# Two weighted rows of a token added on GpSimd instead of in TensorE's transposes, and another order at the end of an attention and expert kernel

## The reference

```python
x = x + xattn(layernorm(x), ctx)        # softmax(q k^T / 8) v, then Wproj and a bias
h = layernorm(x)                        # the second half, per token
probs = softmax(h @ gate_w.T); w2, i2 = top_k(probs, 2)
y = silu(h @ expert_w.T + expert_b)     # of experts i2 alone
x = x + (sum over the two of w2 * y[i2]) @ combine_w.T
```

## Time and profile before

| | |
|---|---|
| time, median of 3 | 1557.53 us (1556.89 to 1558.26) |
| the profiled execution | 1557.89 us, its span 1555.8 us |
| busy | PE 96%, DVE 83%, ACT 68%, POOL 60% |
| chain that ended last | PE 74%, DVE 14%, issue 5% |
| mean granted TensorE clock | 0.995 of full |

### The profile page before, as it was taken

The page is one execution under the profiler, slowest core; times in us unless marked ns, Lnnn a source line. Parts: engine busy times, 40 slices in busy tenths (PEclk is TensorE's granted clock), DMA queues, the critical chain, the costliest instruction groups (busy, mean ns, idle before and its releaser), DMA issues.

```text
span 1555.8 us, 38495 instructions
## 1 busy us (share of the span) xinstructions
PE 1492.6 (96%) x11680; PEld 1436.3 (92%) x11680; DVE 1289.1 (83%) x3129; ACT 1060.4 (68%) x2929; POOL 939.2 (60%) x1237
## 2 busy tenths in 40 slices
PE   6989999999999999999999999999999999999778
PEld 6889999999899999999899999989999999999767
DVE  7898888888888888888988888888888888877556
ACT  5766777777667766677667677667776766767545
POOL 4666666666555655687766555576676556655524
PEclk9999999999999999999999999999999999999989
DMA  6643433333577777445687777657888877877813
GB/s 194 194 149 96 120 96 96 96 96 101 165 227 232 215 222 219 120 127 145 189 246 237 207 221 226 177 159 227 246 243 242 243 215 238 267 224 226 292 58 109
DMA packets 181595, 287.78 MB, mean 185 GB/s; under 512 B 23696, under 2 KB 116880, under 8 KB 181136
## 3 DMA queue, kind: packets, MB, share of 16 engines
q1 hardware_dynamic: 170640, 255.94, 56.4%
q0 software_dynamic: 10752, 29.37, 6.0%
HBM read 156.51 MB, written 61.60 MB: 140 GB/s over the span
## 4 chain that ended last, share of the span: by engine, by line
PE 74%; DVE 14%; issue 5%; ACT 2%; POOL 2%; DMA 2%; SPq 0%; DVEq 0%; ACTq 0%; POOLq 0%
PE gen_ps L592 19%; PE qk_ps L592 17%; PE o_ps L592 10%; PE s_ps L592 9%; PE proj_ps L592 9%; PE pT_ps L633 6%; DVE sums L1070 2%; PE gen_ps L711 2%; DVE pT_s_lo L1005 2%; DVE neg_max L1063 2%; DVE qk_s L1005 1%; PE gen_ps L678 1%; PE gen_ps L686 1%; DMA k_s<-qk_s 1%; DVE xn L1050 1%
## 5 line engine op out<-in xcount | busy, mean ns | idle before, releaser
L848 ACT ACTIVATE stage<-s_ps,neg_max 128x128 f32<-128x128 f32 x1024 | 292.8, 375 | 31.9 <-DVE neg_max L1063 31.4
L1402 POOL CAST o_s_hi<-stage 128x256 fp32r<-128x256 f32 x256 | 102.5, 400 | 342.6 <-ACT stage L822 340.3
L1393 POOL TENSOR_TENSOR stage<-stage,inv_sums 128x512 f32<-128x512 f32 x256 | 266.3, 1040 | 36.5 <-DVE inv_sums L1072 36.1
L822 ACT CAST qk_s<-qk_ps 128x512 fp32r<-128x512 f32 x256 | 150.4, 587 | 136.6 <-PE qk_ps L592 134.9
L1063 DVE TENSOR_REDUCE neg_max<-s_ps 128x4 f32<-128x512 f32 x256 | 176.3, 689 | 68.1 <-PE s_ps L592 64.6
L592 PE MATMUL s_ps<-k_s,qk_s 128*128 128x256 f32 x1536 | 226.1, 283 | 3.1 <-DMA k_s<-qk_s 2.5
L1005 DVE TENSOR_TENSOR pT_s_lo<-pT_ps,pT_s_hi 128x512 fp32r<-128x512 f32 x256 | 173.6, 678 | 43.4 <-ACT pT_s_hi L822 39.5
L592 PEld LDWEIGHTS s_ps<-k_s,qk_s 128*128 128x128 f32 x1536 | 201.2, 189 | 3.9 <-DMA k_s<-qk_s 3.1
L1404 POOL TENSOR_TENSOR o_s_lo<-stage,o_s_hi 128x256 fp32r<-128x256 f32 x256 | 189.4, 740 | 20.8
L822 ACT CAST v_s_hi<-gen_ps 128x512 fp32r<-128x512 f32 x129 | 75.6, 586 | 178.4 <-PE gen_ps L592 178.4
L822 ACT CAST pT_s_hi<-pT_ps 128x512 fp32r<-128x512 f32 x256 | 150.3, 587 | 63.9 <-PE pT_ps L633 59.7
(11 more groups left out here) (367 smaller groups left out, 4701.0 us busy)
## 6 DMA issues: line engine op xcount, KB each, us to landing
w_block<-expert_table SPq DMA_DIRECT2D x147, 512.0 KB
k_s<-qk_s SPq DMA_DIRECT2D x512, 128.0 KB
stage<-sorted_x SPq DMA_DIRECT2D x147, 128.0 KB
sorted_y<-stage SPq DMA_DIRECT2D x147, 128.0 KB
x_raw<-in_x SPq DMA_DIRECT2D x32, 256.0 KB
c_raw<-in_ctxT SPq DMA_DIRECT2D x32, 256.0 KB, 3.8
stage<-in_x SPq DMA_DIRECT2D x32, 256.0 KB
x_kept<-x SPq DMA_DIRECT2D x32, 256.0 KB, 3.8
```

The source lines that it names most:

```text
L822: last = act.copy(to, of)
L848: last = act.activation(probs[p % 2][:, k, :], s_ps[:, k * P:(k + 1) * P], ACT.Exp, bias=neg_max[p % 2][:, k:k + 1])
L1393: pool.tensor_tensor(probs[b][:, :, :], probs[b][:, :, :], inv_sums[b][:, :].unsqueeze(2).broadcast_to([P, 4, P]), ALU.mult).then_inc(prob ...
L1402: pool.tensor_copy(hi[:, :, :], o_full).then_inc(o_hi, 1)
```

## The change

Six edits. (1) For the sparse pairs that are weighed in a slot before 248 (`added_first`: 21 of them) GpSimd adds the two weighted rows of each token, one instruction of 128x512 (`add_rows`), in the slot after the weighing, and `turn_mixed` becomes four plain transposes. (2) For these, the turn, the combine, `combined`, the read-back and the store all come one slot later; for the others they stay (`mix_turn`). `got` is laid out so that the two rows stand 512 elements apart. (3) A third place for the dense results (`over_chosen`). (4) DVE does `expert_out` and `combined` ahead of the dense work of a slot. (5) GpSimd takes a slot's `add_odd` and `gather` in turn, one of each. (6) `load_experts(1)` is issued a slot later, in 256.

```diff
+        self.added_first = [r for at, r in sorted(self.mix.items()) if at < SLOTS * (pairs - 1)]
+        self.mix_turn = {at + (2 if r in self.added_first else 1): r for at, r in self.mix.items()}
...
-            if s - 1 in self.mix:
-                mid.append(("turn_mixed", self.mix[s - 1]))
+            if s in self.mix_turn:
+                mid.append(("turn_mixed", self.mix_turn[s]))
...
-            if s - 2 in self.mix:
-                late.append(("combine", self.mix[s - 2]))
+            if s - 1 in self.mix_turn:
+                late.append(("combine", self.mix_turn[s - 1]))
...
+        over_chosen = flat_stage[:, taken[0] - 8 * E * max(CHUNKS):taken[0]][:, 0:2 * C]
...
-        y_all = [y[:, :, :].rearrange("p t n -> p (t n)") for y in (x_raw, c_raw)]
+        y_all = [y[:, :, :].rearrange("p t n -> p (t n)") for y in (x_raw, c_raw)] + [over_chosen]
...
-                if s == SLOTS * pairs - 1:
+                if s == SLOTS * pairs:
                     load_experts(1)
...
-                        pe.wait_ge(weighted, m + 1)
-                        mm = turn_sum(lambda t, k: got[m % 2][:, 2 * t + k, :], bank)
+                        if n in plan.added_first:
+                            pe.wait_ge(rows_added, n + 1)
+                            mm = turn(got[m % 2][:, 0:2, :], bank)
+                        else:
+                            pe.wait_ge(weighted, m + 1)
+                            mm = turn_sum(lambda t, k: got[m % 2][:, t + 2 * k, :], bank)
...
-                wait(dve, dense_added, n - 1)
-                wait(dve, dense_scaled, n - 1)
-                wait(dve, dense_pooled, plan.pooled(n - 1))
-                dve.scalar_tensor_tensor(out=y_all[n % 2], in0=th_all[n % 2], scalar=1.0,
+                wait(dve, dense_added, n - Y_PLACES + 1)
+                wait(dve, dense_scaled, n - Y_PLACES + 1)
+                wait(dve, dense_pooled, plan.pooled(n - Y_PLACES + 1))
+                dve.scalar_tensor_tensor(out=y_all[n % Y_PLACES], in0=th_all[n % 2], scalar=1.0,
...
+                if s - 2 in plan.turn:
+                    expert_out(plan.turn[s - 2][2])
+                if s - 2 in plan.mix_turn:
+                    combined(plan.mix_turn[s - 2])
                 todo = plan.dense.get(s - 1, [])
...
-                if s - 2 in plan.turn:
-                    expert_out(plan.turn[s - 2][2])
-                if s - 3 in plan.mix:
-                    combined(plan.mix[s - 3])
...
+            def add_rows(m):
+                pool.wait_ge(weighted, m + 1)
+                first, second = (got[m % 2][:, k:k + 2, :].rearrange("p t c -> p (t c)") for k in (0, 2))
+                pool.tensor_tensor(first, first, second, ALU.add).then_inc(rows_added, 1)
...
-                for n in plan.dense.get(s - 1, []):
-                    if n % DENSE_JOBS >= 2:
+                if plan.mix.get(s - 1) in plan.added_first:
+                    add_rows(plan.pair_of[plan.mix[s - 1]])
+                for n, mk in zip_longest(plan.dense.get(s - 1, []), plan.gather.get(s, [])):
+                    if n is not None and n % DENSE_JOBS >= 2:
                         add_odd(n)
-                for m, k in plan.gather.get(s, []):
-                    gather(m, k)
+                    if mk is not None:
+                        gather(*mk)
```

More of the change, by code:

```diff
@@ L1 @@
 from contextlib import ExitStack
+from itertools import zip_longest
 import concourse.bass as bass
@@ L31 @@
 DENSE_PER_SLOT = 3
+Y_PLACES = 3
 RING = 3
@@ L354, in xattn_moe_kernel @@
         ctx_rest = sem("ctx_rest")
-        ctx_lo, probs_done, weighted = (
-            sem(n) for n in ("ctx_lo", "probs_done", "weighted"))
+        ctx_lo, probs_done, weighted, rows_added = (
+            sem(n) for n in ("ctx_lo", "probs_done", "weighted", "rows_added"))
         eps_done = [sem(f"eps_done{n}") for n in (1, 2)]
@@ L934, in weigh @@
                 for k in range(4):
-                    last = act.activation(got[m % 2][:, k, :], got[m % 2][:, k, :], ACT.Copy, scale=top_w[:, m, k:k + 1])
+                    rows = got[m % 2][:, k // 2 + 2 * (k % 2), :]
+                    last = act.activation(rows, rows, ACT.Copy, scale=top_w[:, m, k:k + 1])
                 last.then_inc(weighted, 1)
```

17 lines of the change are left out of this document (9 added, 8 removed).

## The result

| | before | after |
|---|---|---|
| time, median of 8 runs each | 1558.76 us (1556.89 to 1562.45) | 1545.81 us (1542.53 to 1552.82) |
| ratio | | 0.9921, 95% interval 0.9906 to 0.9937 |
| the profiled execution | 1557.89 us, its span 1555.8 | 1546.37 us, its span 1544.6 |

Faster by 0.8%, or 12.3 us by the ratio, where 24.1 were forecast; the time lies above the range of 1526 to 1542. Six of the eight runs after lie between 1542.5 and 1546.4 us, two at 1552.4 and 1552.8.

A forecast was written before the change was run, and what follows sets the result against it. TensorE, busy 96% of the span, was taken as the bound, with waits and a low clock at the end. 1557.9 - 9.5 (attention) - 15.0 + 1.5 - 1.1 = 1533.8, less the median's 0.4: 1533.4 us, range 1526 to 1542.

The forecast's parts named there:

- 84 transposes: Attention's 21 mixed turns: four transposes less in each, 0.099 to 0.109 us apiece on a saturated TensorE, 9.0 us gained.
- the turn a slot later: Attention: the value product's waits for `expert_out` in u = 2 go, -1.5; new waits on the bank `combined` frees, +1.0.
- 21 additions on GpSimd: Attention: 1.3 us each, 27.3 us on GpSimd, taken as covered and costed at 0.
- end: order, last store, small waits: The end: `expert_out` first removes waits and low clock, -15.0; last store earlier, -1.1; small waits of the chain, +1.5.
- end: third place: The end: a third place for dense results frees DVE, as job 6 needs job 3's addition; no separate size.
- end together: The whole end: -15.0 for waits and clock, -1.1 for the last store, +1.5 for small waits.
- the split ahead of the projection in u = 3: Attention: 1.21 us of room against a 1.3 us addition, projection moving back 1.0; cost 0, else 0.1 to 1.3 each.
- The port rule: DVE instructions with two SBUF inputs and GpSimd's SBUF reads share ports; each addition could hold DVE up to its length.
- By the row it is 0.36: The one measured port hold: `dense_add` on DVE takes 0.84 us beside GpSimd's addition, 0.48 alone.
- B (gathers): The end: GpSimd's gathers still pace the dense chain and half of the 15 comes back; 1541 us, chance 0.12.
- A: Slot 258: the experts' second half lands late, TensorE waits up to 3.4 us, low clock returns; 1539.4 us, chance 0.09.
- Rival D: Projections of u = 1 and u = 3: additions hold TensorE up, 1.66 us each; slower, 1568 us, chance 0.03.

The follow-up runs named there:

- noadd4: The changed kernel without GpSimd's additions, its moved turns of four transposes on the first row alone (second expert's share left out): 1535.59 us, ratio 0.985.
- shift8: The changed kernel with the 21 turns still a slot later, but of eight transposes and without GpSimd's additions: 1543.37 us, ratio 0.9903.
- end_only: The kernel before with the edits of the end alone, no turn moved and no rows added on GpSimd: 1539.16 us, ratio 0.9871.
- out_behind: The edits of the end alone, but with `expert_out` and `combined` behind the slot's dense work again: 1552.82 us, ratio 0.9957.
- two_places: The edits of the end alone, but with two places for the dense results as before: 1545.23 us, ratio 0.9917.
- weights4: The changed kernel with only VectorE's `top_w` of the sparse pairs moved from u = 0 to u = 4: 1541.69 us, ratio 0.9893.
- addlate: The changed kernel with GpSimd's addition moved behind the split of the next slot: 1548.84 us, ratio 0.9932.
- add_same: The changed kernel with the turns of four in their old slots and GpSimd's addition at the end of the weighing's slot: 1540.01 us, ratio 0.9878.
- write_only: The changed kernel with each GpSimd addition replaced by a memset of the same rows (experts' share left out): 1540.49 us, ratio 0.989.

## Why the prediction was wrong, point by point

| step | forecast | measured |
|---|---|---|
| 84 transposes | -9.0 | -7.8 (noadd4 against shift8) |
| the turn a slot later | -1.5 + 1.0 | +4.2 (shift8 against end_only; +2.5 by the traces) |
| 21 additions on GpSimd | **0** | **+10.2** (after against noadd4; +11.7 from slot 128 by the traces) |
| end: order, last store, small waits | -15.0 - 1.1 + 1.5 | -13.7 (out_behind against end_only) |
| end: third place | no term of its own | -6.1 (two_places against end_only) |
| end together | -14.6 | -18.7 (end_only against before) |

**The step that failed is the additions' cost of 0.** The prediction looked for cover in the wrong place. It put the danger on GpSimd's queue (the split ahead of the projection in u = 3) and found 1.21 us of room, and no wait of TensorE for that split showed, right so far. The port rule was weighed too, and set aside with two reasons that both fail. "By the row it is 0.36": that row was of two instructions of like length, one of which had started 0.16 us ahead of the other. How long VectorE is held depends on what is left on GpSimd, not on VectorE's instruction: in the kernel before `top_w` takes 0.38, 0.61 and 0.94 us where 0.35, 0.58 and 0.91 us of the bias addition are left (pairs 10, 12, 25). The rule that was weighed named only instructions with two SBUF inputs, and `rounded` has one. And "most of VectorE's work in u = 0 reads PSUM, and it has 7.6 us free in a pair": true of the busy time, but one instruction of 0.16 us is enough, where what TensorE waits for stands behind it. The evidence was in the trace of before: `top_w` with a mean of 809 ns for 4 numbers a partition, next to an alone time of 0.16. Here a mean that didn't fit the size marked a hold. The prediction didn't list VectorE's groups by that measure.

What the 10.8 us that the additions cost between slots 128 and 248 are made of, by the table: 3.4 lie in the six plain pairs and 6.8 in the three counting pairs. With `top_w` out of the way 1.5 and 0.7 of these go, and 1.1 in the other pairs, which is the clock in pair 23 (720.9 to 717.6, 3.3 in all). Of the 7.4 that are left above noadd4, 6.1 lie in the three counting pairs (151.5 against 145.4), 1.9 in the plain pairs, and the others, where nothing differs, give -0.6. In the three counting pairs `rounded` is held for 2.97 to 3.23 us, and in 27 and 29 the clock falls behind it, in weights4 too (0.59 in the stretch behind the 2.11 us). These two pairs are 2.7 and 2.4 us longer than in noadd4; in addlate, with waits of 2.23 and 2.22 us and the clock at 1.00, they are 1.4 and 1.1 longer. So about half of their loss is the clock. No run moved `rounded` by itself, so that its hold starts the 6.1 is argued from the traces, not shown.

The 1.9 was not taken apart by a run. In the trace of weights4 it shows as a wait of 0.20 to 0.23 us for the probabilities' low part in u = 4 of pairs 18, 19, 24 and 25. Ahead of it VectorE's layernorm, two `tensor_scalar` in u = 3, takes two to three times as long beside GpSimd's next instructions, which the second addition has made about 1.2 us later. Pair 25 in weights4, pair 26, which has no such wait, and pair 25 in noadd4:

```profile
1131.92 2.12 DVE L1062 TENSOR_SCALAR xn<-x,mv,rstd 128x255 f32<-128x255 f32 x2
```

```profile
1181.99 1.48 DVE L1062 TENSOR_SCALAR xn<-x,mv,rstd 128x255 f32<-128x255 f32 x2
```

```profile
1132.58 0.72 DVE L1062 TENSOR_SCALAR xn<-x,mv,rstd 128x255 f32<-128x255 f32 x2
```

So by the traces an addition costs in two ways: by what it holds, and by moving the rest of GpSimd's queue beside other instructions of VectorE.

**The shift.** The forecast saw the wait for `expert_out` in u = 2 go, and it did (0.15 us in each plain pair), but a wait for the probabilities' low part, 0.4 us, came in u = 0 of pairs 19, 25 to 27 and 29, where the turn of eight had covered that chain. In pair 27 the turn itself took over the wait, 1.16 us even without an addition, in place of 0.64 and 0.49. And the last pair lost 2.5. The +1.0 was a wait on `combined` that did not show.

**The transposes** were sized well, 0.093 each where the prediction had 0.099 to 0.109. They were not hidden.

**The end** was right in its mechanism and order, and 4.1 too small together. Undone one at a time the two edits cost 13.7 and 6.1, 19.8 against 18.7 together (11.5 and 4.9, 16.4 against 18.8, from slot 128 by the traces), so no run shows that they overlap. The order came out at about what was forecast for it (14.6); the third place, which the sum had no term for, is what was missing. Of the rivals, B (gathers) did not come in the changed kernel: VectorE still waits up to 1.06 us for GpSimd's additions there, but TensorE at most 0.34 us for VectorE. A did not come: dense job 4 ran at 1477.24, and TensorE has no wait for a weight. The later load was not tried by itself, nor was taking additions and gathers in turn.

**Rival D** had the right resource, the port pair, at the wrong place and with a chance of 0.03. Its price of 1.66 for each addition was three times too high (0.49): only eight of the 21 additions made a hold of `top_w` or `rounded` longer. The room at the projection of u = 3, on which the forecast looked, was 0.83 to 0.90 us in the plain pairs of the changed kernel, where it had been 1.21.

## What to carry to other kernels

Before work is added to GpSimd, list VectorE's instructions beside the new place that read SBUF alone, however small, and ask who waits for what stands behind them; a 128x4 instruction was held through two of GpSimd's additions, 2.6 us. Look in the profile for instructions whose mean doesn't fit their size: here 809 ns in the mean against 0.16 us was there to be seen, and moving that one instruction gave 2 to 4 us in the changed kernel. Where VectorE ran no such instruction beside it, in the plain pairs of add_same, the addition cost nothing. And judge an edit that merges two ideas by running each alone: this one's gain was all in one of them.

## What the runs showed of the hardware

- VectorE is held through two GpSimd instructions back to back, not only through the one that runs when it comes: `top_w` 2.77 us and `rounded` 2.97 us, both through 1.28 and 1.29. The Trainium skill, "SBUF — State Buffer", section "Who interferes with whom", says that who issues first keeps the pair for its whole instruction; the measured hold is longer than one instruction. It isn't the whole queue either: the cast that starts 0.05 us before the bias addition's end doesn't hold them further.
- A `tensor_scalar` on 9 numbers a partition is held by a memset as well, which reads nothing (2.64 us through a memset of 0.97 and an addition of 1.30). `top_w`, with two inputs, takes 0.16 us right ahead of the same memset.
- An instruction that is held counts as busy, from its own start: the kernel after has 14.6 us more of VectorE's busy time for the same 3129 instructions.
- A memset of 128x1024 takes 0.957 us on GpSimd, an addition of 128x512 1.287 (means of 21).
- After a wait of 2.41 us TensorE's granted clock was 0.51 for three microseconds in the middle of attention, where the kernel before has waits of 0.64 and 0.49 us and matmuls at the full level behind both. The length of the wait alone doesn't settle it: at the same place the clock fell behind 2.11 us (weights4) and stayed at 1.00 behind 2.23 (addlate) and 2.06 (write_only).
